# attention_1: another order of head 0's opening products, two of the four row scalings out of PSUM on VectorE, four values chunks ahead of the head loop

## What is computed

```python
x = x + _L1_attn_ref(_layernorm(x, axis=-1), wq, bq, wk, bk, wv, bv, wo, bo, ln_g, ln_b)

x = (h - mu) * jax.lax.rsqrt(var + EPS) * ln_g + ln_b
q = (x @ wq.T + bq).reshape(b, s, N_HEADS, D_K)      # k, v alike
q = rope(q); k = rope(k)
attn = jnp.einsum('bihd,bjhd->bhij', q, k) * scale
attn = softmax(where(causal, -inf, attn))
o = jnp.einsum('bhij,bjhd->bihd', attn, v).reshape(b, s, N_HEADS * D_K)
return o @ wo.T + bo + residual
```

## Time and profile before

| | |
|---|---|
| median of 3 runs | 1021.83 us (1020.08 to 1021.9) |
| the profiled execution | 1013.77 us |
| its span | 1012.0 us |
| PE busy | 964.2 us (95% of the span) |
| DVE, ACT, POOL busy | 718.1, 597.6, 419.2 us |

### The profile page before, as it was taken

How to read it: one execution, slowest core, us unless ns; L and a number is a source line. 1 busy time by engine, 2 the same in 40 slices (tenths; PEclk the granted TensorE clock), 3 DMA queues, 4 the chain that set the end, 5 groups by cost and what they waited for, 6 DMA issues and landing times. The chain is left out here.

```text
span 1012.0 us, 20916 instructions
## 1 busy us (share of the span) xinstructions
PE 964.2 (95%) x7030; PEld 798.7 (79%) x7033; DVE 718.1 (71%) x2160; ACT 597.6 (59%) x1515; POOL 419.2 (41%) x408
## 2 busy tenths in 40 slices
PE   8899999999998998999999899999999998899988
PEld 7677878777875654877778789988898887788877
DVE  6777777777764568663457678777787785669994
ACT  2178777777775675232224777777777764235333
POOL 5777666766664201145513344344343461110000
PEclk9999999999999999999999899999999999999999
DMA  5360222022000200652230401101010000001111
GB/s 184 68 217 12 64 53 55 22 64 43 2 1 20 94 1 2 218 146 84 78 115 7 153 17 31 36 18 39 26 34 23 28 10 1 1 1 48 48 38 52
DMA packets 27640, 54.53 MB, mean 54 GB/s; under 512 B 4534, under 2 KB 14902, under 8 KB 25846
## 3 DMA queue, kind: packets, MB, share of 16 engines
q1 hardware_dynamic: 25350, 47.44, 16.1%
q0 software_dynamic: 2208, 6.03, 2.0%
HBM read 38.90 MB, written 6.16 MB: 45 GB/s over the span
## 5 line engine op out<-in xcount | busy, mean ns | idle before, releaser
L532 ACT ACTIVATE sb_a_P<-sb_a_nS,sb_a_nm 128x257 f32<-128x257 f32 x256 | 127.6, 507 | 84.7 <-DVE sb_a_nm L643 84.6
L442 POOL TENSOR_TENSOR sb_a_P<-sb_a_P,sb_a_rec 128x512 f32<-128x512 f32 x128 | 129.2, 1040 | 85.9 <-DVE sb_a_rec L654 85.8
L643 DVE CUSTOM_DVE_ANT_0 sb_a_nS<-a_pS,sb_a_mask,sb_a_nsink 128x256 f32<-128x256 f32 x256 | 109.3, 478 | 38.0 <-PE a_pS L791 38.0
L2276 ACT ACTIVATE sb_a_t<-a_pp,sb_a_w 64x512 f32<-64x512 f32 x124 | 84.7, 683 | 13.8 <-PE a_pp L144 6.4
L2202 POOL TENSOR_TENSOR sb_a_qT<-sb_a_t 128x512 f32<-128x512 f32 x32 | 41.3, 1289 | 107.6 <-DVE sb_a_t L2365 107.6
L2362 DVE SCALAR_TENSOR_TENSOR sb_a_t<-a_pp,sb_a_w,sb_a_cs 128x512 f32<-128x512 f32 x62 | 46.2, 746 | 53.5 <-ACT sb_a_t L2276 53.5
L144 PE MATMUL a_pp<-sb_x_high,sb_a_w_low 128*128 128x512 f32 x182 | 78.3, 430 | 3.9 <-DVE sb_a_P L598 3.6
L144 PE MATMUL a_pp<-sb_x_high,sb_a_w_high 128*128 128x512 f32 x182 | 72.3, 397 | 0.0
L144 PE MATMUL a_pp<-sb_x_low,sb_a_w_high 128*128 128x512 f32 x182 | 72.3, 397 | 0.0
L541 ACT COPY sb_xn<-a_pT 128x512 f32<-128x512 f32 x128 | 67.9, 582 | 1.9 <-PE a_pT L805 1.9
L805 PE MATMUL a_pT<-sb_ident,sb_a_P 128*128 128x128 f32 x512 | 68.2, 276 | 0.3 <-ACT sb_xn L541 0.3
(11 more groups left out here) (493 smaller groups left out, 2895.9 us busy)
## 6 DMA issues: line engine op xcount, KB each, us to landing
sb_a_kr<-sb_a_kall SPq DMA_DIRECT2D x28, 256.0 KB, 4.3
sb_f_w<-f_w SPq DMA_DIRECT2D x12, 384.0 KB, 3.1
sb_a_w<-a_w SPq DMA_DIRECT2D x16, 257.0 KB, 2.6
sb_m_egu<-m_egu SPq DMA_DIRECT2D x2, 1408.0 KB, 9.1
sb_a_w<-a_w SPq DMA_DIRECT2D x8, 259.0 KB, 2.7
sb_a_wo<-a_wo SPq DMA_DIRECT2D x8, 256.0 KB, 2.7
sb_a_wv<-a_wv SPq DMA_DIRECT2D x8, 256.0 KB, 2.6
sb_a_wo<-a_wo SPq DMA_DIRECT2D x16, 128.0 KB, 2.0
```

Source lines behind the costliest of these rows:

```text
L442: nc.gpsimd.tensor_tensor(part, part, rec[b % 2][:, h, :].rearrange("p (q o) -> p q o", o=1) .to_broadcast([P, 2, S]), ALU.mult).then_inc( ...
L532: out = nc.scalar.activation(Pm[b % 2][:, h, qt, 0:S + 1], nS[:, h, qt, 0:S + 1], ACT.Exp, bias=nm[b % 2][:, h, qt:qt + 1], scale=-1.0, ac ...
L643: out = nc.vector.tensor_tensor_reduce(nS[:, h, qt, 0:S], pS[h][:, qt * S:(qt + 1) * S], wmask[:, qt, :], -1.0, nsink[par][:, h:h + 1], AL ...
L2276: out = nc.scalar.activation(turned_half[a, :, :].rearrange("p b s -> p (b s)"), bank[b, :], ACT.Identity, bias=bias[b])
```

## The change

It has three parts. First, the scaling of quarters 2 and 1 is done by DVE (`row_by_vector`), 0 and 3 stay on ACT; before, DVE did quarter 1 alone, in other words quarter 2 moves. On DVE quarter 2 stands behind the statistics, and quarter 1 ahead of chunk 0's rope instead of behind it. Second, PE turns the last rows ahead of chunk 2 instead of behind it, and ACT scales and rounds them between the swaps of chunks 0 and 2. Third, all four values chunks of heads 0 and 1 come from the opening: chunk 4 ahead of chunk 1, and 5, 6 and 7 behind chunk 3. 6 and 7 go to `pp[0]` and `pp[1]`; so head 1's chunks 0 and 1 now wait for DVE to have taken them, and head 0's slots 2 and 3 have no chunk. Two of `grow`'s eight tiles move behind the swaps of chunks 1 and 3.

```diff
--- before.py
+++ after.py
@@ -2051,7 +2051,7 @@
         pY = k.ps(ctx, "a1_pY")
         turn_banks = [pS[0], pS[1], pT, pO[0]]
         first_banks = {0: pp[0], 2: pp[1], 4: pY, 5: pO[1], 1: pS[0], 3: pT}
-        PROJECTED, ROTATED = [0, 2, 4, 5, 1, 3], [0, 2, 1, 3]
+        PROJECTED, ROTATED = [0, 2, 4, 1, 3, 5, 6, 7], [0, 2, 1, 3]
         sem = lambda name: k.sem("a1_" + name)
         gate = sem("gate")
@@ -2128,6 +2128,10 @@
             return isinstance(X, int) and X == 0
+        def early_values(X, c):
+
+            return isinstance(X, int) and X == 1 and c >= 6
+
         def turn_of(X, c):
             return ROTATED.index(c) + 1 if opening(X) else X * 4 + c + 1
@@ -2135,13 +2139,17 @@
         CHUNKS = {1: {0: (0, 1), 1: (2, 3), 2: (4,), 3: (5,)},
                   0: {0: (0, 1), 1: (2, 3), 2: (6,), 3: (7,)}}
-        def chunks(par, b, last, drain):
-            return () if last or drain else CHUNKS[par][b]
+        def chunks(par, b, first, last, drain):
+            if last or drain or (first and b >= 2):
+                return ()
+            return CHUNKS[par][b]
         def filled(X, c):
-            if opening(X):
+            if opening(X) or early_values(X, c):
                 return PROJECTED.index(c) + 1
+            if isinstance(X, int) and X == 1:
+                return len(PROJECTED) + c + 1
             return X * 6 + (c + 1 if c < 6 else c - 1)
         block = ctx.enter_context(nc.Block(no_gpsimd_drain=True))
@@ -2235,7 +2243,7 @@
             def w_to_high(X, par):
                 w_arrived(act, X, par)
-                act.wait_ge(proj, 6 if isinstance(X, int) and X == 2 else (X - 2) * 6 + 4)
+                act.wait_ge(proj, len(PROJECTED) if isinstance(X, int) and X == 2 else (X - 2) * 6 + 6)
                 high_of(nc, ws[par][0][:, :], w[par][:, 0:2 * KD * P]).then_inc(w_high, 1)
             def wo_to_high(H, par):
@@ -2279,7 +2287,7 @@
             def step(H, par, first=False, last=False, drain=False):
                 for b in range(A1_U if not drain else 1):
-                    cc = chunks(par, b, last, drain)
+                    cc = chunks(par, b, first, last, drain)
                     if exists(H, b, 1, first, drain):
                         h, u, _ = after(H, b, 1)
                         act.wait_ge(turnedP, h * A1_U + (u + 1))
@@ -2313,21 +2321,21 @@
                         high_of(nc, OT[u % 2][0][:, :], pO[u % 2][:, 0:2 * P]).then_inc(OT_high, 1)
             turned_row(0)
-            turned_row(2)
-            act.wait_ge(affine, 2)
+            act.wait_ge(affine, 1)
             high_row(0)
+            act.wait_ge(affine_by_vector, 1)
             high_row(2)
             swap(0, 0, 0)
+            turned_row(3)
+            act.wait_ge(affine_by_vector, 2)
+            high_row(1)
+            act.wait_ge(affine, 2)
+            high_row(3)
             swap(0, 0, 2)
-            turned_row(3)
-            act.wait_ge(affine_by_vector, 1)
-            high_row(1)
-            act.wait_ge(affine, 3)
-            high_row(3)
-            grow(range(0, 3))
+            grow(range(0, 1))
             swap(0, 0, 1)
             swap(0, 0, 3)
-            grow(range(3, NT))
+            grow(range(1, NT))
             heads(act, step)
         @block.vector
@@ -2346,7 +2354,14 @@
                 nc.vector.scalar_tensor_tensor(out=shift[:, cols], in0=k.mv[:, cols, 0], scalar=-1.0, in1=root2[:, 0, cols],
                                                op0=ALU.mult, op1=ALU.mult).then_inc(shifts, 1)
+            def row_by_vector(j):
+                d = j // NH2
+                dve.wait_ge(turned, j % NH2 + 1)
+                nc.vector.tensor_scalar(part_of(k.xT, j), turn_banks[j][:, :], cols_of[:, 0, d:d + 1], cols_of[:, 1, d:d + 1],
+                                        ALU.mult, ALU.add).then_inc(affine_by_vector, 1)
+
             row_stats(nc, dve, k, k.x, first_head.ln, 0, 1)
+            row_by_vector(2)
             low_row(0)
             low_row(1)
             shift_rows(0)
@@ -2439,18 +2454,18 @@
                         add_y(h, u)
                     ready = cc[1:]
+            row_by_vector(1)
             rope(0, 0, 0)
-            dve.wait_ge(turned, 2)
-            nc.vector.tensor_scalar(part_of(k.xT, 1), turn_banks[1][:, :], cols_of[:, 0, 0:1], cols_of[:, 1, 0:1],
-                                    ALU.mult, ALU.add).then_inc(affine_by_vector, 1)
             low_row(2)
             low_row(3)
             rope(0, 0, 2)
+            values(0, 4)
             shift_rows(1)
             rope(0, 0, 1)
             rope(0, 0, 3)
-            values(0, 4)
             values(0, 5)
+            values(1, 6)
+            values(1, 7)
             heads(dve, step)
             dve.wait_ge(added, A1_H * A1_U)
@@ -2480,8 +2495,12 @@
                 bank = first_banks[c] if opening(X) else pp[c % 2]
                 if c < 2:
-                    if not before(X, c, 2):
+                    if isinstance(X, int) and X == 1:
+                        pe.wait_ge(v_ready, c + 3)
+                    elif not before(X, c, 2):
                         pe.wait_ge(v_ready, X * 2 + (c - 1))
+                elif early_values(X, c):
+                    pe.wait_ge(taken, c - 5)
                 elif not opening(X):
                     pe.wait_ge(taken, X * 4 + (c - 1 if c < 6 else c - 3))
                 if c == 0:
@@ -2569,12 +2588,14 @@
                         weigh(h, par ^ x, u)
             first_chunk(0)
+            turn_half(nc, pe, k, turn_banks, xn_ready, 0, turned, 1)
             chunk_of(0, 0, 2)
-            turn_half(nc, pe, k, turn_banks, xn_ready, 0, turned, 1)
             chunk_of(0, 0, 4)
-            chunk_of(0, 0, 5)
             first_chunk(1)
             chunk_of(0, 0, 3)
+            chunk_of(0, 0, 5)
+            chunk_of(1, 1, 6)
+            chunk_of(1, 1, 7)
             heads(pe, step)
```

## The result

| | median of the runs | runs |
|---|---|---|
| before | 1021.20 us | 18 |
| with the change | 1019.57 us | 18 |

The ratio is 0.998, with a 95% interval of 0.9972 to 0.9989: about 2.0 us faster, between 1.1 and 2.9. The forecast was 1017.7 us, in a range of 1015.5 to 1020.3; the direction and the range held, the gain was forecast at twice its size. A second series (12 runs of the changed kernel, 23 of before) gave 1019.96 against 1021.74 us, ratio 0.9983 (0.9972 to 0.9994).

What follows compares the result with a forecast made beforehand. PE was taken to bound the loop over heads. The terms 0.9 + 2.4 - 0.7 + 1.5 gave 4.1 us, carried to the runs' median of 1021.83 for 1017.7 us, range 1015.5 to 1020.3.

Steps and rivals of the forecast that it cites:

- What bounds it: Loop over heads: PE, busy 99.82 of 100 us, sets the time, so its first steps' gain lasts to the stage's end.
- Chunk 0, 0.5 us: Opening: with the second scaling on DVE, chunk 0 starts behind the filler at 546.4 instead of 546.91, 0.5 us sooner.
- Up to the last key chunk, 1.9 us: Opening: one values chunk fewer ahead of chunks 1 and 3, so the last swap ends 1.9 us sooner, near 555.9.
- a bound, priced at 0.5: Ahead of chunk 1: the last quarter's low part caught behind POOL's first addition, another 0.5 us, leaving 0.4 at first scores.
- DVE and POOL behind it, 1.0 us given back: Before first scores: the small scaling waits for POOL, chunk 1's rope starts 1.0 us late, 0.9 of 1.9 us left.
- rival (b): Before first scores: the small scaling isn't held up; 1.0 us more gain, 5.1 in all, 1016.7 us; chance 0.13.
- The first slot, 2.4 us: Head 0's first slot: the pause shrinks to 1.6 us, the clock holds, and matmuls and scores save 2.4 us.
- Slot 2, 0.7 back: Head 0's second slot: PE waits for banks that ACT and DVE free, giving 0.7 us back.
- Slots 3 and 4, 1.5 us: Head 0's third and fourth slots: each loses a values chunk of 1.36 us; half is taken, 1.5 us for both.
- (a): Pause before first scores: the clock falls in the shorter pause too; 2.5 us gain left, 1019.3 us; chance 0.20.
- (c): First steps: the gain is made but not passed on, something besides PE paces them; 1021.8 us; chance 0.08.
- (d): Slots emptied of chunks: PE pauses in each, the low clock stays over the step, slower at 1024.4 us; chance 0.04.

Runs made afterwards that it cites:

- POOL held: The changed kernel, with POOL's first addition held until the last low part is written; first scores 17.22 us behind the first turning, against 17.57.
- The filler experiment: The kernel before, with 18 filler matmuls in the pause ahead of head 0's first scores; 1019.14 against 1021.74 us, ratio 0.9973.

## Why the prediction was right, and by how much it was off

*What bounds it.* Right: PE paces the loop, and what is won by head 1 is kept. From the turning to the first matmul of the next block it was 306.31 us before and 303.18 with the change, 3.1 less. 0.45 of that came after head 1's start: 0.28 in head 2's second slot (5.42 us before, 5.14 with the change, 5.40 with the scaling back on ACT), the rest in small steps. The cause is not shown.

*Chunk 0, 0.5 us.* It was 0.67 (3.84 to 3.17): the filler is what it starts behind, as forecast. The record of a matmul that follows the filler starts 0.13 before the filler's modelled end, which I had taken for a fence.

*Up to the last key chunk, 1.9 us.* This step failed. The last swap ended 13.87 us behind the turning (564.46 plus 1.38, less 551.97), before 14.73 (557.80 less 543.07): 0.9 us. PE reached chunk 1 1.85 us sooner (8.47 against 10.32), but waited 0.77 us in it for a low part that was caught behind POOL's first addition; ACT, which I had watched for, did not make it wait. With that addition held, the last swap ends 1.79 us sooner than before (12.94): the walk was right but for this meeting. I had named it as a bound, priced at 0.5, and it was the case, at 0.93: the moment could be read from my own walk, where the swap of chunk 0 is through at 549.4, DVE's rope by about 551.1 (an estimate, from its two rows of 0.75 and 0.68), and POOL's addition and the low parts both begin there.

*DVE and POOL behind it, 1.0 us given back.* The mechanism was right, and the small scaling was held up as forecast (0.87 us for 128 by 4 elements; rival (b) falls). What it cost in the changed kernel was less, 0.42 us: from the last swap's end to the first scores it is 3.70 us, before 3.28. The first meeting had already made the swaps late, and the two delays overlap. Where the first is removed (POOL held), that stretch is 4.28 us, and the 1.0 given back is there as forecast. Together 0.44 us were left at the first scores, where I had 0.9 and a lower bound of 0.4; that the bound comes so close is partly luck, since the first meeting cost more than I had priced and the second less. One row behind this forecast was the wrong one: the earlier trace rows shows the read of an accumulator, and the copy of two elements that the text speaks of is this, which ends at 32.65, 0.03 us after POOL's instruction in the earlier trace rows:

```profile
32.12 0.53 DVE L629 COPY sb_a_nS<-sb_a_nsink 128x2 f32<-128x2 f32 x1
```

*The first slot, 2.4 us.* It was 2.34. The pause was 1.05 us, shorter than the 1.6 forecast, since PE's own wait had moved into chunk 1.

*Slot 2, 0.7 back.* It was 0.9. The filler experiment, with nothing else changed, shows the same 0.9: the cost of coming to the banks sooner.

*Slots 3 and 4, 1.5 us.* This term was mis-sized: 0.48 and 0.31, 0.8 together. The emptied slots last as long as the chain through ACT and DVE (3.2 to 3.4 us in all nine profiles of kernels that empty them; PE's waits of 0.65 and 0.55 us above are for these engines), not half way between it and PE's work.

The sum by head 1 was 2.7 us instead of 4.1. Of the rivals, (a), a fall of the clock in the shorter pause, was not seen in any of the nine profiles with a pause between 0.7 and 2.0 us there; it is not excluded, for elsewhere, ahead of the next block, the pause of 1.65 us is followed by a fall in four of the twelve. (c) falls, since the stage's end came sooner by more than head 1 did, and (d) falls with the clock at 1.00 in the emptied slots. The median, 1019.57 us, lies nearest to the 1019.3 of rival (a), whose mechanism did not occur, and 0.6 us of its distance from the forecast come from the base, where 18 runs have a median of 1021.20 and the first three had 1021.83. That the range held says little for the terms.

The runs give about 2 us where the stage gives 3.1, just outside their interval. The granted clock of the runs shows where a part may go. The fall ahead of head 0's scores kept PE at the low level for 6.8 us in both profiles of before (559 to 567 us in the first), 0.0033 of the mean clock of the span. In the second series the mean over the runs is 0.9912 for before and 0.9947 for before with filler, higher by about that much. But it is 0.9913 for the changed kernel, and 0.9924 in its first 18 runs. So its executions have some 4 to 7 us more at the low level elsewhere (an estimate, from these means). Every other fall in the twelve profiles lasts 3.4 us, so that is one to two falls more in an execution, each worth at most 1.7 us, half its length. Why they are more frequent stays open: 22 of the 37 such falls in the profiles lie ahead of the stage, in code that is the same.

## What to carry to other kernels

A pause long enough to drop TensorE's clock costs twice, and filling it with anything, even matmuls into a free bank, returns the second part; try this first, because it needs no new order. When work is moved out of later slots to fill it, ask what those slots last without it: they shrink to the chain of the other engines and no further. And when an order is packed more tightly, check which of VectorE's SBUF-to-SBUF instructions now meet GpSimd's: a small one can be moved to where its engine waits, and GpSimd can be made to wait for a large one that is due.

## What the runs showed of the hardware

**When DVE meets an addition of POOL, the one that comes second waits until the first is through.** A scaling of 128 by 4 elements took 0.16 us alone and 0.87 beside an addition of 128 by 512, and ended 0.01 us after it; a product took 0.68 alone and 1.34 beside it, and ended 0.55 us after POOL's. Beside the low part that was already running, POOL's addition took 1.60 instead of 1.30. DVE's first product of `rope`, with one input in PSUM, took its 0.75 us beside POOL too (at 561.25 in the kernel with POOL held, POOL's addition from 561.06). And not every instruction of POOL holds DVE: in the changed kernel, beside POOL's 128 by 4 TENSOR_TENSOR from 555.46 (1.33 us), the small scaling at 555.81 took 0.16.

**The same pause drops the clock in one execution and not in another.** Before 47.96 us PE paused for 2.53 us in the first profile of before, and the clock stayed. The same place in the changed kernel's profile, with a pause of 2.52 us before 48.69, in a window of 1 us:

```profile
50.00:51.00 1.00, 1.00 (x6) 0.52 (x8) 0.29 (x1) 0.00 (x0) 1.00 (x1) 0.50 0.20 27
```

The clock is at 0.50. Of the twelve profiles, six show a fall there. The Trainium skill says in "TensorE: Matmul & The Clock Gate" (part 1) of the clock's rise that its moment varies from run to run; here it is the fall that comes in one execution and not in another. The pause of 4.7 us dropped the clock in both profiles that had it. Such falls elsewhere in the kernel, from two to five in a profile, go with a scatter of the runs by some us (in the second series, before's three runs with a mean clock of 0.988 took 1024.1 us on average, its five with 0.993 1020.7), which hides a gain of this size.
